# Gates spread to all partitions by eight transfers from their on-chip rows, in place of a store to DRAM and broadcasts back

## The reference

```
logits = xf @ Wr + br                                   # 8 experts per token
topk_w, topk_idx = jax.lax.top_k(logits, TOP_K)         # TOP_K = 2
topk_w = jax.nn.softmax(topk_w, axis=-1)
gate = jnp.sum(jax.nn.one_hot(topk_idx, 8) * topk_w[..., None], axis=1)   # (tokens, 8)
h = jax.nn.relu(jnp.einsum('th,ehf->etf', xf, W1) + b1[:, None, :])       # 128 -> 256 per expert
y = jnp.einsum('etf,efh->eth', h, W2) + b2[:, None, :]                    # 256 -> 128
out = jnp.einsum('te,eth->th', gate, y)
```

## Time and profile before

| | us |
|---|---|
| median of 3 runs | 338.03 (336.07 to 340.14) |
| profiled execution, its own time | 336.87 |
| its span, first to last instruction | 335.0 |
| PE busy | 323.0 (96%) |
| DVE busy | 280.8 (84%) |
| ACT busy | 165.7 (49%) |
| POOL busy | 171.1 (51%) |
| mean granted TensorE clock | 0.995 |

### The profile page before, as it was taken

One profiled execution on the slowest core, in us unless ns is written; L12 is line 12 of the kernel. 1 busy time (PEld: TensorE's weight loads), 2 busy tenths in 40 slices (PEclk: granted clock), 3 DMA queues, 4 the chain that ended last, 5 costly groups with the idle time before them and its releaser, 6 DMA issues.

```text
span 335.0 us, 5104 instructions
## 1 busy us (share of the span) xinstructions
PE 323.0 (96%) x1767; PEld 258.4 (77%) x1767; DVE 280.8 (84%) x800; ACT 165.7 (49%) x303; POOL 171.1 (51%) x173
## 2 busy tenths in 40 slices
PE   7989989999999999999999999999999989999996
PEld 7769756887787868786888778786878668777995
DVE  6796696999699987999699969998779958887874
ACT  1542426555546554563755564754547363346542
POOL 6440550588427853487347842785408832435440
PEclk9999999999999999999999999999999997999999
DMA  4770004100250006100520025000610034004201
GB/s 132 243 203 0 2 0 153 72 1 0 81 204 3 0 6 249 31 1 2 201 85 0 0 78 210 0 2 2 250 34 0 0 115 171 1 1 179 75 2 31
DMA packets 13456, 23.62 MB, mean 71 GB/s; under 512 B 1764, under 2 KB 8087, under 8 KB 12407
## 3 DMA queue, kind: packets, MB, share of 16 engines
q1 hardware_dynamic: 13202, 23.17, 20.4%
q10 hardware_dynamic: 164, 0.07, 0.1%
q0 software_dynamic: 64, 0.07, 0.1%
HBM read 21.07 MB, written 2.23 MB: 70 GB/s over the span
## 4 chain that ended last, share of the span: by engine, by line
PE 78%; DVE 8%; DMA 5%; POOL 3%; ACT 2%; issue 2%; SPq 1%; DVEq 0%; POOLq 0%
PE bank L1109 9%; PE bank L1125 8%; PE bank L1111 8%; PE bank L1110 8%; PE bank L1135 8%; PE bank L1126 8%; PE bank L1039 6%; PE bank L1024 3%; PE bank L972 3%; DMA gate_bc<-gates_d 2%; DMA br_bc<-in_L_ffn_br_dram 2%; PE bank L1154 2%; PE bank L987 2%; PE bank L1146 1%; PE bank L1160 1%
## 5 line engine op out<-in xcount | busy, mean ns | idle before, releaser
L468 POOL TENSOR_TENSOR hg_lo<-hg,hg_hi 128x512 fp32r<-128x512 f32 x65 | 87.7, 1358 | 73.7 <-ACT hg_hi L521 73.7
L521 ACT ACTIVATE hg_hi<-hg 128x512 fp32r<-128x512 f32 x128 | 79.8, 628 | 77.9 <-DVE hg L852 76.7
L852 DVE SCALAR_TENSOR_TENSOR hg<-bank,neg_b,gate_bc 128x512 f32<-128x512 f32 x128 | 94.2, 741 | 25.1 <-DMA gate_bc<-gates_d 14.0
L1109 PE MATMUL bank<-h_hi,w_hi 128*128 128x512 f32 x128 | 58.5, 457 | 1.5 <-ACT gate_rows L563 1.5
L1125 PE MATMUL bank<-hg_hi,w_hi 128*128 128x512 f32 (+1 forms) x144 | 53.8, 374 | 0.0
L1135 PE MATMUL bank<-hg_lo,w_hi 128*128 128x512 f32 (+1 forms) x144 | 53.4, 371 | 0.0
L1126 PE MATMUL bank<-hg_hi,w_lo 128*128 128x512 f32 (+1 forms) x144 | 53.1, 369 | 0.0
L1111 PE MATMUL bank<-h_lo,w_hi 128*128 128x512 f32 x128 | 50.8, 397 | 0.0
L1110 PE MATMUL bank<-h_hi,w_lo 128*128 128x512 f32 x128 | 50.7, 396 | 0.0
L865 DVE TENSOR_TENSOR hg_lo<-hg,hg_hi 128x512 fp32r<-128x512 f32 x63 | 47.4, 752 | 1.1 <-ACT hg_hi L521 0.6
L437 POOL TENSOR_SCALAR var_eps<-mv 128x4 f32<-128x4 f32 x16 | 4.0, 251 | 66.7 <-DVE mv L598 66.7
(11 more groups left out here) (168 smaller groups left out, 557.0 us busy)
## 6 DMA issues: line engine op xcount, KB each, us to landing
gate_bc<-gates_d SPq DMA_DIRECT2D x8, 1024.0 KB, 7.0
gate_bc<-gates_d SPq DMA_DIRECT2D x8, 512.0 KB, 5.0
gate_bc<-gates_d SPq DMA_DIRECT2D x14, 256.0 KB, 3.6
out_dram<-x_all SPq DMA_DIRECT2D x7, 256.0 KB, 2.3
w_raw<-in_L_ffn_W_dram SPq DMA_DIRECT2D x1, 1024.0 KB, 8.5
x_all<-in_L_attn_x_dram SPq DMA_DIRECT2D x2, 256.0 KB, 4.2
wmod_sb<-in_L_wmod_dram SPq DMA_DIRECT2D x1, 384.0 KB, 4.9
out_dram<-x_all SPq DMA_DIRECT2D x2, 128.0 KB, 1.9
```

The lines of the kernel that those rows point to most:

```text
L468: g.tensor_tensor(hg_lo[k][:, :], hg[k][:, :], hg_hi[k][:, :].bitcast(fp32), ALU.subtract).then_inc(s_lo_pool, 1)
L521: a.activation(hg_hi[k][:, :], hg[k][:, :], ACT.Copy).then_inc(s_hghi, 1)
L852: v.scalar_tensor_tensor(hg[k][:, :], up_bank[n % 4][:, :], neg_b1[:, n:n + 1], gate_bc[own % 2][:, n // NU, :], ALU.max, ALU.mult).then_i ...
L1109: t_.matmul(dst, w_hi, hx, start=True, stop=False)
```

## The change

The tensor `gates_d` in DRAM, the store to it and the semaphore of the store are gone. `gates_out(b)` now waits for `gate_rows`, and then issues one transfer per expert, each of which reads one partition of `gate_rows` (512 values, 2 KB) and writes it to all 128 partitions of `gate_bc` (256 KB). These are eight transfers per row, seven for rows 0 and 7, 62 in all, where there were 8 stores and 30 loads. The four semaphores stay, and count one transfer per expert of their chunk. ACT, ahead of overwriting `gate_rows`, now waits for the transfers of the previous row that read it.

```diff
-        gates_d = nc.dram_tensor("gates_d", [B, E * T], fp32).ap()
...
-        s_gst = sem("s_gst")
...
             def gates_out(b):
 
-                sp.wait_ge(s_grow, b + 1)
-                sp.dma_start(gates_d[b].rearrange("(e t) -> e t", e=E), gate_rows[0:E, :]).then_inc(s_gst, 16)
                 if b >= 2:
                     sp.wait_ge(s_hg, (b - 1) * N)
-                sp.wait_ge(s_gst, 16 * (b + 1))
+                sp.wait_ge(s_grow, b + 1)
                 for k, (lo, hi) in enumerate(CHUNKS):
                     if k == 0 and b in FIRST_GATE_BANK:
                         continue
-                    sp.dma_start(gate_bc[b % 2][:, lo:hi, :].rearrange("p e t -> p (e t)"),
-                                 gates_d[b, lo * T:hi * T].partition_broadcast(P)).then_inc(s_gbc[k], 16)
+                    for e in range(lo, hi):
+                        sp.dma_start(gate_bc[b % 2][:, e, :], gate_rows[e:e + 1, :].unsqueeze(1).to_broadcast([1, P, T])).then_inc(s_gbc[k], 16)
...
                         if m1 >= 1:
-                            act.wait_ge(s_gst, 16 * m1)
+                            for c, (lo, hi) in enumerate(CHUNKS):
+                                if c or m1 > 1:
+                                    act.wait_ge(s_gbc[c], 16 * (hi - lo) * (m1 if c else m1 - 1))
                             act.wait_ge(s_glo, m1)
...
                         elif n in [NU * lo for lo, hi in CHUNKS]:
-                            dve.wait_ge(s_gbc[[NU * lo for lo, hi in CHUNKS].index(n)], 16 * (own + 1))
+                            c = [NU * lo for lo, hi in CHUNKS].index(n)
+                            dve.wait_ge(s_gbc[c], 16 * (CHUNKS[c][1] - CHUNKS[c][0]) * (own + 1))
```

## The result

The changed kernel takes 781.44 us (median of 4 runs, 780.7 to 783.46), against 337.62 us for the kernel before: a ratio of 2.317, with an interval of 2.308 to 2.326. The forecast was 793 us, with a range of 490 to 1090 us. The profiled execution has a span of 780.2 us. All ratios are of fast runs: a run that is over 1.5% above the fastest of the same kernel is left out of them.

What follows compares the result with a forecast made beforehand. PE was taken to bound the kernel before; after the change, row 0's start, six turns of 95.0 us and the last row's transfers and work, plus 1.87 us outside the span, made 793 us, range 490 to 1090 us.

Steps and rivals of the forecast that it cites:

- first issue to tile 8, eight transfers: Each full row: 2.5 us fixed time plus eight transfers of 9.53 us, 76.2 us, before DVE's tile 8.
- tile 8 to the next issue: Each row: 14.6 us of work that can't lie beside the transfers, with 1.7 us for the clock counted per turn.
- DVE's wait for gates: DVE waits at tiles 0, 2, 4 and 8 of each row, for 450 us in all.
- PE's busy share: Over the whole kernel, PE would be busy for some 40% of the time.
- The price of the read: Each 256 KB spread from one partition takes 9.53 us, all 16 engines sharing one group's 27.5 GB/s; 62 such transfers count.
- The fixed time: About 2.5 us per transfer beside its bytes, from the 256 KB and 1024 KB loads; counted once per row's transfers.
- The turn as a loop: Next row's gates come after this row's tile 8, so two rows' transfers can't overlap: 95.0 us per turn, formerly 36.3.
- ACT's new waits: ACT's waits for the transfers cost nothing, since by tile 13 DVE has used every transfer that they name.
- The clock: After each long wait PE's clock stands at half for 3.4 us, which loses 1.7 us, counted once per turn.
- The issues: SP's eight issues per row take some 5 us, with nobody behind them but the output store.
- Two doors at once: Rival, chance 0.08: experts 0 to 3 and 4 to 7 use different doors together, 4.8 us per transfer, 497 us.
- The source doesn't matter: Rival, chance 0.15: on-chip transfers behave as the loads did, 1.1 us each, some 3 us gained, 334 us.

Runs made afterwards that it cites:

- late4: The kernel before with experts 4 to 7 spread from their on-chip rows, 0 to 3 still loaded from DRAM: 524.73 us, ratio 1.561.
- the probe: Transfers alone, no kernel work: eight 256 KB spreads in the changed kernel's order, four from partition 0, then four from partition 4: 76.6 us.
- nostore: The kernel before without the store to DRAM and its wait, the four loads reading another DRAM input: ratio 0.994.
- alternate: The changed kernel with SP's issues in the order of experts 0, 4, 1, 5, 2, 6, 3, 7: 577.95 us in one run.
- eightloads: The kernel before with eight 256 KB loads from DRAM per row in place of four, store kept: ratio 1.0006.

## Why the prediction was right

By its own steps, against the profiled execution:

| step | predicted | measured |
|---|---|---|
| first issue to tile 8, eight transfers | 78.7 us | 77.0 us |
| tile 8 to the next issue | 16.3 us | 16.2 to 17.8 us, mean of six 16.9 |
| tile 8 of row 0 at | 121.2 us | 120.05 us |
| turn, mean of six | 95.0 us | 93.9 us |
| row 7, tile 8 to tile 8 | 81.4 us | 79.5 us (683.42 to 762.91) |
| tile 8 of row 7 to the end | 18.4 us | 17.3 us |
| DVE's wait for gates | some 450 us | 446.6 us |
| PE's busy share | some 40% | 52% |

- **The price of the read** was the step on which all hung, and it held. The fullest window of the 16 engines gave 27.5 GB/s per group; one group delivers 27.3. The lower rate of the output store (18.4 GB/s) was the wrong row. That the engines hide their gaps behind one another, my reason for that choice, fits but was not tested.
- **The fixed time** was mis-sized: 1.6 us, not 2.5. That it was too large because the 1024 KB loads partly queue behind others is argued and not shown. It makes 7 us (eight rows of 0.9 us) of the 12 us that the forecast was too high, but terms of both signs stand beside it. 62 transfers at 9.6 in place of 9.53 us are 4 us more; the rows still came 1.4 to 1.9 us each under 1.6 us + 9.6 us per transfer, 12 us less in all (see two doors below); and the stretches from tile 8 to the next issue took 3.6 us more than counted. The 12 us are small because these partly cancel.
- **The turn as a loop** (the gates of the next row can't be made before tile 8 of this one) held, and `late4` shows it at another size. There the forecast was 10 to 25 us too high, because the four spreads start among the loads. ACT's new waits cost nothing, as forecast: the profile shows no wait of ACT for these transfers.
- **The clock** came out near by luck. I counted 3.4 us at half clock, which costs 1.7. PE was idle from 194 to 213 with the granted clock at 0.50, and the clock stayed at half (1.2 GHz) in all of the window from 213 to 226 (busy time of PE, PEld, DVE, ACT and POOL, then the granted clock, the DMA share and GB/s). In the rows 0 to 6 it came back to full 10 to 13 us after the start of tile 8:

```profile
213.00:226.00 13.00, 11.40 (x35) 9.20 (x36) 10.52 (x36) 4.88 (x9) 7.59 (x6) 0.50 0.01 2
```

The stretch from tile 8 to the next issue still grew only from 14.6 to 16.9 us, by 2.3 where I had 1.7. DVE was busy for 10.5 of these 13 us, and PE had made the up-projections of the tiles 8 to 11 while DVE waited; that these two made up for the clock is argued and not shown. The forecast of PE's busy share, some 40%, left the clock out (323.0 us of 793); the mean 128x512 matmul with the low part of the weights took 469 ns in place of 396, and the share was 52%.
- **The issues** were costed at some 5 us per row. They took 55.36 us: the first two 0.5 and 0.6 us, the third 6.8 us, the later ones 8.9 to 9.6 us, each held while two or three spreads were on the way. It cost next to nothing, because only the output store stands behind them; it lands after 22.3 us, where it took 2.3 before.
- **Two doors at once** had 0.08, on the argument that each engine takes its queue in order. The order of the eight issues alone brings 578 us, so both doors can be used at once, in part. In the changed kernel's own order the four sources of a group follow one another, and only the change from one group to the other gains something: 76.6 us in the probe and 77.0 in the kernel, where 1.6 + 8 x 9.6 is 78.4. The rival was wrong for this order, and my reason against it was too strong.
- **The source doesn't matter** had 0.15 and 3 us of gain. Its gain was about right (`nostore`: 0.6%); its condition isn't met, by a factor of four or more per transfer (9.6 us against the 2.1 to 2.4 us that a row can bear).

## What to carry to other kernels

Ask of a spreading transfer how many partitions it reads, not only how many bytes it moves: in a row of transfers 256 KB took 1.1 to 1.4 us from DRAM or straight across the partitions, and 9.6 us from one partition. Before removing a detour, price what is late because of it (here 0.6% of the time), and hold the new path's time against the moment at which each piece is needed: one such transfer per row behind 35 us of cover cost under 1%, eight per row more than doubled the time. Where such reads can't be avoided, neighbours in the queue should read different groups: that took the changed kernel from 781 to 578 us.

## What the runs showed of the hardware

- A group of on-chip partitions delivers 27.3 GB/s to all 16 DMA engines together. 0, 1 and 32 are of one group, 4 and 64 of others.
- The engines take a queue of one order but not in step: four transfers of 256 KB from two groups in turn took 28.3 us, sixteen of 64 KB 21.7 us, with the same bytes; one group alone took 40 us either way. In the long pieces the first lands as if alone, and later ones 4.7 us apart, with two groups (`alternate`) as with eight.
- A slow source shows as busy DMA engines: a share of 0.9 at 27 GB/s. The share alone doesn't tell work from waiting.
- An issue is held when spreads from on-chip rows pile up: 0.59 us for a lone one, 9.6 us for the later ones of a row, with three on the way. Spreads of 64 KB, which land nearly as fast as one alone, were issued one per 0.90 us. Eight loads from DRAM were issued in 3.64 us, one per 0.46 us, with six on the way (`eightloads`).
- After DVE's waits of 25 to 29 us ahead of tile 8 (PE idle from 194 to 213 in row 1) the clock stayed at 1.2 GHz for 10 to 13 us, with PE busy for 11.4 of 13.0 us in row 1; it stayed there for 3.4 us after the short wait in the kernel before.
